# A branch hint for the back edge of TensorE's loop in a recurrent-cell kernel

## The reference, cut to what matters

```python
Xz, Xr, Xh = X @ Wxz.T + bxz, X @ Wxr.T + bxr, X @ Wxh.T + bxh     # for all steps
def step(H, xs):
    xz, xr, xh = xs
    Z = sigmoid(xz + H @ Whz.T + bhz)
    R = sigmoid(xr + H @ Whr.T + bhr)
    H_tilda = tanh(xh + R * H @ Whh.T + bhh)
    H_new = Z * H + (1.0 - Z) * H_tilda
    return H_new, H_new @ Whq.T + bhq
_, Ys = scan(step, h0, (Xz, Xr, Xh))
x = x + transpose(Ys)
```

## Time and profile before

| | |
|---|---|
| three runs, us | 581.74, 580.05, 582.3 (median 581.74) |
| the profiled execution's own time, us | 582.49 |
| its span, first to last instruction, us | 580.4 |
| mean granted TensorE clock | 0.988 |
| PE busy / weight loads busy | 556.9 us (96%) / 545.5 us (94%) |
| VectorE busy / ScalarE busy | 322.7 us (56%) / 289.6 us (50%) |

### The profile page before, as it was taken

The page is one execution under the profiler, slowest core; times in us unless marked ns, Lnnn a source line. Parts: engine busy times, 40 slices in busy tenths (PEclk is TensorE's granted clock), DMA queues, the critical chain, the costliest instruction groups (busy, mean ns, idle before and its releaser), DMA issues.

```text
span 580.4 us, 105994 instructions
## 1 busy us (share of the span) xinstructions
PE 556.9 (96%) x49372; PEld 545.5 (94%) x49372; DVE 322.7 (56%) x1802; ACT 289.6 (50%) x1671; POOL 0.2 (0%) x4
## 2 busy tenths in 40 slices
PE   7599999999999999999999999999999999999996
PEld 6589999999999999999999999999999999999996
DVE  1145555555555655555655555555555555555554
ACT  2145555545545555555455554554555555555553
POOL 0000000000000000000000000000000000000000
PEclk9599999999999999999999999999999999999999
DMA  4011111111111111111111111111111111111111
GB/s 154 17 35 48 41 50 45 41 52 43 45 50 41 49 46 42 52 42 45 50 41 49 45 41 50 45 45 50 41 46 49 41 50 45 45 50 41 47 48 46
DMA packets 57880, 27.58 MB, mean 48 GB/s; under 512 B 7056, under 2 KB 56976, under 8 KB 57872
## 3 DMA queue, kind: packets, MB, share of 16 engines
q1 hardware_dynamic: 56736, 26.63, 16.2%
q10 hardware_dynamic: 1136, 0.83, 0.4%
HBM read 18.91 MB, written 8.52 MB: 47 GB/s over the span
## 4 chain that ended last, share of the span: by engine, by line
PE 96%; issue 3%; DMA 0%; DVE 0%; ACT 0%; SPq 0%; DVEq 0%; ACTq 0%
PE r_ps L232 38%; PE c_ps L232 25%; PE z_ps L232 22%; PE y_ps L232 11%; DMA xres_sb<-in_xt_dram 0%; DVE o_sb L199 0%; SPq L122 0%; ACT c_ps L147 0%; DVE u_sb L218 0%; ACT r_ps L147 0%; ACT c_sb L174 0%; ACT z_ps L147 0%; DVEq L30 0%; DVE ones_sb L185 0%; DVE h_sb L223 0%
## 5 line engine op out<-in xcount | busy, mean ns | idle before, releaser
L232 PE MATMUL c_ps<-xt_sb,wx_sb 128*32 128x64 f32 x4128 | 174.6, 226 | 1.5 <-issue 1.5
L167 ACT ACTIVATE r_sb<-r_ps 128x32 f32<-128x32 f32 x512 | 74.3, 197 | 152.4 <-PE r_ps L232 152.4
L213 DVE TENSOR_TENSOR rh_sb<-r_sb,h_sb 128x32 f32<-128x32 f32 x512 | 75.1, 188 | 101.0 <-ACT r_sb L167 101.0
L232 PE MATMUL r_ps<-u_sb,whr_sb 128*32 128x32 f32 x8192 | 122.0, 198 | 8.9 <-issue 2.6
L232 PE MATMUL r_ps<-zh_sb,whr_sb 128*32 128x32 f32 x8192 | 124.9, 197 | 3.5 <-issue 3.5
L232 PE MATMUL z_ps<-h_sb,whz_sb 128*32 128x32 f32 x8192 | 124.5, 198 | 0.0
L218 DVE SCALAR_TENSOR_TENSOR u_sb<-z_sb,c_sb 128x32 f32<-128x32 f32 x512 | 75.2, 188 | 83.7 <-ACT c_sb L174 83.7
L232 PE MATMUL c_ps<-rh_sb,whh_sb 128*32 128x32 f32 x8192 | 121.7, 198 | 0.0
L232 PEld LDWEIGHTS r_ps<-u_sb,whr_sb 128*32 128x32 f32 x8192 | 103.4, 112 | 19.0 <-issue 19.0
L232 PE MATMUL y_ps<-h_sb,whq_sb 128*32 128x64 f32 x4128 | 118.2, 224 | 0.3 <-DVE o_sb L199 0.3
L232 PE MATMUL z_ps<-xt_sb,wx_sb 128*32 128x64 f32 x4128 | 113.7, 220 | 2.7 <-issue 2.7
(11 more groups left out here) (26 smaller groups left out, 257.5 us busy)
## 6 DMA issues: line engine op xcount, KB each, us to landing
xt_sb<-in_xt_dram SPq DMA_DIRECT2D x130, 64.0 KB, 1.8
xres_sb<-in_xt_dram SPq DMA_DIRECT2D x130, 64.0 KB, 1.8
out_dram<-o_sb SPq DMA_DIRECT2D x130, 64.0 KB, 1.6
wx_sb<-in_wx_dram SPq DMA_DIRECT2D x2, 256.0 KB, 4.3
wx_sb<-in_wx_dram ACTq DMA_DIRECT2D x1, 256.0 KB, 4.9
whz_sb<-in_whz_dram SPq DMA_DIRECT2D x1, 256.0 KB, 5.3
whr_sb<-in_whr_dram ACTq DMA_DIRECT2D x1, 256.0 KB, 6.0
whq_sb<-in_whq_dram SPq DMA_DIRECT2D x1, 256.0 KB, 6.3
```

What stands on the lines that cost most here:

```text
L167: nc.scalar.activation(r_sb[:, o], r_ps[:, o, here], ACT.Sigmoid).then_inc(s_r[o], 1)
L213: nc.vector.tensor_tensor(rh_sb[:, k], r_sb[:, k], old[:, k], ALU.mult).then_inc(s_rh[k], 1)
L232: return nc.tensor.matmul(ps, weights, moving, start=start, stop=False, skip_group_check=True, **kw)
```

## The change: a hint at the top of each pass

```diff
@@ -280,7 +280,7 @@
             pe.wait_ge(s_whq, DMA)
             pe.wait_ge(s_xt[1], DMA)
 
-            with pe.Fori(0, NIT) as i:
+            with nc.Fori(0, NIT, engines=[mybir.EngineType.PE], hint_back_edge=True) as i:
                 for u in range(SLOTS):
                     t = i * SLOTS + u
                     p, s = divmod(u, CS)
```

## The result

The changed kernel takes 592.31 us (median of 4 runs, 589.86 to 593.15) against 581.5 us; the ratio is 1.0182 (95% interval 1.0144 to 1.022). It is slower, as forecast, but by 10.8 us instead of 4.7, just outside the range.

What follows compares the result with a forecast made beforehand. TensorE, busy 96% of the span, was taken to bound the kernel, starved by its sequencer at each back edge; 4.0 us for the hint plus 0.7 at the exit on 581.74 gave 586.4 us, range 580.0 to 592.0.

Steps and rivals of the forecast that it cites:

- Step 1: TensorE's back edge: the loop body stays in instruction memory, so the hint removes no fetch; 0 us.
- The rival by the rule of two cache lines: TensorE's back edge hides a fetch that the hint removes, giving 561.8 us; chance 0.03.
- Nothing hides the added instruction: Top of TensorE's pass: its queue is empty, so the hint's sequencer time shows in full, 4.0 us in all.
- Step 2: Top of TensorE's pass: one added sequencer instruction, 64 times at 0.062 us, costs 4.0 us.
- Step 3: TensorE's loop branch: the same instruction with the same resident target, so 0 us.
- The rival of the cheap branch: TensorE's back edge: the armed hint has already searched for the far block, giving 575.5 us; chance 0.10.
- Step 4: Loop exit: prefetch steered to the head leaves the block behind the loop missing; 0.7 us, from 0 to 1.2.
- Refetching: TensorE's loop: steered prefetch displaces resident blocks, so passes fetch again, 863 us more, 1445 us; chance 0.04.
- The signs: Changed profile: idle 0.32 to 0.34 us, passes 8.66 us, branch 208 ns, at most 7 packets, pause near last y_ps loads.

Runs made afterwards that it cites:

- hint_off: Changed kernel's hint at the top of the pass, but with a register saying not taken, so nothing is steered; 589.11 us, ratio 1.0109 to the kernel before.
- top_add: counters with one register add moved from mid-pass to the top of the pass, just behind the branch; 575.75 us, 0.9882 of the kernel before.
- hint_two: Changed kernel with two hints instead of one for the same branch at the top of the pass; 598.93 us, 1.0267 of the kernel before.
- counters_hint: counters with a hint as the only sequencer instruction at the top of the pass; 578.22 us, 0.9928 of the kernel before.
- end_add: counters with one register add moved from mid-pass to just ahead of the branch; 575.95 us, 0.9895 of the kernel before.
- counters: Kernel before, no hint, back-edge register work replaced by four registers raised in mid-pass; 568.86 us, ratio 0.9769.

## Why the prediction was right or wrong

**No fetch to hide: right.** Step 1 rested on 7 packets and a pause filled with recorded sequencer work. The changed kernel moved 7 packets again, and the doubled body shows what a fetching back edge looks like: 4.1 us, not 0.38. The rival by the rule of two cache lines falls. The Trainium skill, "Runtime: NRT & Kernel Launch", section "Instruction fetch mechanics", says both that TensorE has room for 2048 instructions and that only two lines are held; the runs (seven blocks stay, 13 don't) agree with the first and not with the second.

**Nothing hides the added instruction: right.** This is the mechanism of the forecast, and why its direction held. The same instruction costs 0.163 us a pass at the top, 0.043 at the start of the third step, and 0.015 where TensorE waits anyway.

**Step 2, the price of 0.062 us: wrong, and this is the main miss.** The added instruction costs 0.148 us a pass (0.163 less 0.015 for the branch, next step), some 9 us instead of 4.0. The miss has two parts, an instruction's ordinary price and, the larger one, a surplus that I had no term for.

*The ordinary price* is 0.09 us, and accounts for some 1.5 to 2 us of the miss. I took a record (44 ns) plus the unrecorded rest of the pause (20 ns). Records are not what the sequencer is held for. Measured from start to next instruction, an instruction in that place takes 86 ns (`hint_off`), 88 (`top_add`) or 94 (the register work of the kernel before), whether its record says 28, 36 or 44. The pause misled me: I compared its idle length (0.27 us) with the records, although the same rows gave 0.38 us of lost time, so 0.13 us of sequencer work had no record. The records of before also hold the distance from the register work's start to the first load, 94 ns. At that price step 2 is 6.0 us and the sum 6.7 us, 588.4 us by the prediction's base.

*The surplus* is about 0.06 us a pass. It appears when an armed hint shares the top with another instruction (`hint_two`, both orders in `top_add`'s loop) and hardly alone (`counters_hint`). In the changed kernel it stands between the hint and the register work, 156 ns where an instruction's own price is about 86. Of the 9.8 us that the 62 distances are longer, some 5.5 are the ordinary price, 0.9 the branch and 3.4 this. Its cause was not found.

**Step 3, an unchanged branch: wrong by 0.015 us a pass.** An armed hint makes the taken branch 223 instead of 208 ns: 1 us in all. The rival of the cheap branch has the sign reversed.

**Step 4, the exit: the mechanism right, the size short.** The count of 261 instructions against 256 put the last few beyond the block, and three loads were. I put the cost at 0.7 us between 0 and 1.2; it is 1.9 in this profile (1.4 between the two kernels with 50 warm-up matmuls). Asked for at the last branch, the block was there for the loads at 587.92, 4.0 us later and not 3.7. Counted from the last branch, VectorE's last rows started at 4.4 instead of 3.1 us (588.34 - 583.9, 577.86 - 574.8), 1.4 us late; and from there to the end it was 3.0 instead of 2.5 us, since the last store landed 2.1 us behind its issue instead of 1.6; I had not thought of that. I had also averaged in a zero that my own count spoke against.

**Refetching: no.** The instruction queue moved 7 packets with the hint as without it.

**The signs.** The number of packets and the pause in the last y_ps loads came as described; the idle time (0.44 us, not 0.32 to 0.34), the pass (8.77, not 8.66) and the branch (223, not 208) did not. That the time lies only 0.3 us beyond the range is due to its wide upper bound of 0.15 us a pass, which had no mechanism behind it.

## What to carry to other kernels

In these runs a back-edge hint gained something only where the trace shows the branch waiting for code: a branch record of microseconds and instruction packets in every pass. Where the body stays in instruction memory, what counts at the back edge of a full TensorE is the number of sequencer instructions that stand together. Each costs about 0.09 us there, so keep registers up to date in mid-pass and let the branch stand alone: that took 13 us, 2.3%, off this kernel, with the same matmuls. Price such instructions by start-to-start distances, not by the length of their records.

## What the hardware showed that I had not expected

- At the end of a pass, the first sequencer instruction behind the matmuls starts 6 loads, 0.1 us, ahead of TensorE (3 loads where a hint and an add share the top); a second one right behind it starts only when those loads have started (17 ns behind the last). One add ahead of the branch costs 0.097 us a pass by this alone (`end_add` against `counters`, 8.507 against 8.410), though its record is 32 ns.
- A taken branch holds TensorE's sequencer 263 to 266 ns from start to next instruction, ScalarE's 166 and SyncE's 164 in the kernel before. The Trainium skill, "Advanced Engine Details and Errata", section "Control Flow Timing", gives about 108 ns for a compare-and-branch; none of these agrees.
- An armed hint at the top or in the third step keeps the block behind the loop from being fetched until the loop is left; one at the end of the pass doesn't. The exit took 7.2 to 8.0 us with such a hint, 1.4 to 2.4 us more than in the kernel before or in its own twin, even where the hint costs nothing in the passes. (Without a hint on TensorE it took 5.6 to 6.9 us, and the two longest of these also fetched a block there.)
- A block that is fetched while a data transfer is on its way at the exit goes with a transfer of 2.3 to 3.2 us instead of 1.7 to 1.9, with a hint or without.
- The 0.05 to 0.07 us of an armed hint in company is unexplained.
